# VectorE's attention loop turned at unit 6 of a group instead of at the group's end

## The chip, the cores and the metric

The kernel runs on one core of a Trainium2 chip. A NeuronCore has engines that run programs of their own and meet through semaphores: TensorE (PE in the profile; matmuls and transposes, PEld its weight loads), VectorE (DVE), ScalarE (ACT), GpSimd (POOL) and SyncE (SP, which issues DMAs). The metric is the device time of one launch in microseconds; less is better.

## The reference, cut to what matters

```python
x = x + _L0_cond_ref(...)     # a 32x32 weight picked per batch
x = x + _L1_cond_ref(...)     # base weight, bias, a LoRA adapter per batch
x = x + _L2_cond_ref(...)     # attention, below
x = x + _L3_cond_ref(...)     # as L0
...
def _L2_cond_ref(x, Wq, Wk, Wv, Wo, q_norm_w, k_norm_w, k_cache, v_cache, block_table, cache_seqlens):
    q, k = _rope(_rmsnorm(q, q_norm_w), pos), _rope(_rmsnorm(k, k_norm_w), pos)
    k_all = jnp.concatenate([k_cache[block_table], k], axis=1)   # 512 cached + 32 own rows
    v_all = jnp.concatenate([v_cache[block_table], v], axis=1)
    scores = jnp.einsum('bqhd,bkhd->bhqk', q, k_all) * SCALE
    probs = jax.nn.softmax(jnp.where(valid, scores, -1e30), axis=-1)
    o = jnp.einsum('bhqk,bkhd->bqhd', probs, v_all)
    return jnp.einsum('bse,de->bsd', o, Wo)
```

x is 64 batches of 32 rows by 512. There are 32 query heads and 8 key/value heads of 128; four query heads with 32 rows each share a key head, which makes 128 rows of scores.

## The kernel before

The stages run one after the other: the first two residual steps, the projections (v, then q and k, to about 720 us of the trace), the attention (about 720 to 2090 us), and the second half of the output projection with the last residual step.

**The attention** is a pipeline over units. One unit is one batch and one key head: 64 batches by 8 heads are 512 units. A group is four batches, 32 units (UG), and there are 16 groups (NT), 0 to 15. Every engine has its own list of `step(g, u)` calls. Each engine writes group 0 out, loops over groups 1 to 14, and writes group 15 out. PE, ACT and DVE turn their loops after unit 31. POOL's loop runs from unit 24 to unit 23 of the next group (ROT). SP's body is one call of `group`. SP reaches its turn when units 2 and 3 of the next group are being worked on, since it waits for outputs of the group's last batch.

For unit n of a group, DVE's step n does, in this order: `split_k` for unit n+3 (the low part of the keys, k_lo, L999), `masked_max` for n+2 (L1013, L1014; nmx), `inverse` (L1020) and `normalise` (L1025, L1026) for n+1, and at some units a mask (L991), a q split (L1005), the low part of the outputs (`heads_low`, L1031), and at unit 31 the residual sum (L1037). PE's step n computes scores of n+2 (L1247), which need k_lo of n+2 and the maximum of n. It turns the probabilities of n (L1134), which needs DVE's L1026 of that unit, and multiplies with the values of n-1 (L1280, with L1290 at the end of a batch). ACT's step n does the exponential of n+1 (L744), the high part of the keys of n+4 (k_hi, L730), and the copy of the turned probabilities (L790). After each batch come L768, L751 and L753.

**SP** loads the key pages of batch b+2 into the buffer of batch b as soon as DVE has made the last k_lo of batch b: it waits at L445, then issues own keys (L383), reads 16 page numbers and issues 16 loads of 128 KB (L378). The queries (L387) go ahead of these. Then come own values (L392), the store of outputs (L456) and, in the fourth batch, x2's store (L465). ACT's L730 is the first to read the pages, four units ahead of PE.

Waits are on counters that count on through the program, so the place of a loop's turn changes no dependency.

Of the kernel before, what the change touches and what calls it, by code (L numbers as in the profile page):

```python
# [43 lines left out]
UG = BT * HK  # L44
# [13 lines left out]

HEADS_AT = {2: (1, 3, 0), 5: (1, 0, 1), 6: (1, 1, 1), 8: (1, 2, 1), 10: (1, 3, 1), 18: (0, 0, 0), 21: (0, 1, 0), 26: (0, 2, 0)}
RESIDUAL = UG - 1  # L60
WO_SPLIT = 8

SCALE = 1.0 / float(np.sqrt(D))
# [16 lines left out]
def build(nc, x, cond_row, id_row, bt_row, idx_pages, seq_tok, seq_all, w0, w3, wb, bias,  # L80
# [3 lines left out]
    with ctx:  # L84
# [224 lines left out]
        def _(sp):  # L309
# [9 lines left out]
            def load_b(i, j):  # L319

                i, j, t = tile(i, j)
                _, rows = nc.values_load_multi_w_load_instructions(
                    ids[0:1, bass.ds(t * BT, BT)], engines=SP, min_val=0, max_val=LORAS - 1)
                for b in range(BT):
                    sp.dma_start(b4[j][b * RANK:(b + 1) * RANK, :],
                                 lora_b[bass.ds(rows[b], 1)].rearrange("a r n -> r (a n)")).then_inc(s_bin[j], 16)
# [47 lines left out]
            def load_pages(table, par, first=0, count=NPP):  # L374

                _, pages = nc.values_load_multi_w_load_instructions(table, engines=SP, min_val=0, max_val=PAGES - 1)
                for n in range(count):
                    sp.dma_start(k_sb[par][:, first + n, :, :].rearrange("p h t -> p (h t)"),  # L378
                                 kT_cache[bass.ds(pages[n], 1)].rearrange("a p n -> p (a n)")).then_inc(s_k[par], 16)
# [229 lines left out]
        def _(act):  # L609
# [160 lines left out]
            def split_wo(half, h, raw):  # L770

                if h == 0:
                    act.wait_ge(s_wo_in, 16 * half + 16)
                at = slice(h * T, (h + 1) * T)
                nc.scalar.copy(wo_hi[:, at], raw[:, at]).then_inc(s_wohi, 1)

            def step(g, u):
                n = g * UG + u
                fixed = isinstance(n, int)
                if u % HK == 0 and not (fixed and n == 0):  # L780
                    own_turned(g * BT + (u // HK - 1))
                if u % HK == 1 and not (fixed and n == 1):
                    out_heads(*((g, u // HK - 1) if u > 1 else (g - 1, BT - 1)))
                if not (fixed and n + 1 >= NU):
                    exps(n + 1, u + 1)
                if u % HK != 1 and not (fixed and n + 4 >= NU):
                    split_k(n + 4, u + 4, g * 2 + (u + 4) // (2 * HK))
                act.wait_ge(s_ta, n + 1)
                ge(act, s_pv, n - 1)
                nc.scalar.copy(pT_sb[u % 2], pT).then_inc(s_evA, 1)  # L790
                if u % HK == 1 and not (fixed and n + 4 >= NU):
                    split_k(n + 4, u + 4, g * 2 + (u + 4) // (2 * HK))
                if u % 4 == 3 and not (fixed and n + 5 >= NU):
                    split_q(g * (UG // 4) + (u // 4 + 2), u + 5, g * 2 + (u + 5) // (2 * HK))
                if u in HEADS_AT:
                    back, b, half = HEADS_AT[u]
                    if not (fixed and g < back):
                        heads_high(g - back, b, half)
# [18 lines left out]
            for u in range(UG):  # L817
                step(0, u)
                if 0 <= u - WO_SPLIT < H2:
                    split_wo(0, u - WO_SPLIT, wo_raw)  # L820
            with act.Fori(1, NT - 1) as g:
# [32 lines left out]
        def _(dve):  # L854
# [134 lines left out]
            def make_mask(b):  # L989

                nc.vector.tensor_scalar(mask[:, 0:L], iota[:], seqf[:, bass.ds(b, 1)], NEG, ALU.is_ge, ALU.mult)\  # L991
                    .then_inc(s_mask, 1)

            def split_k(n, u):

                b, h = u // HK % 2, u % HK
                dve.wait_ge(s_khi, n + 1)
                lo, hi = (k[u % 2].rearrange("p (s t) -> p s t", t=PSIZE) for k in (k_lo, k_hi))
                nc.vector.tensor_tensor(lo, k_sb[b][:, :, h, :], hi.bitcast(F32), ALU.subtract).then_inc(s_klo, 1)  # L999

            def split_q(m, u):

                b, h, i = u // HK % 2, u % HK, u // 4 % 2
                dve.wait_ge(s_qhi, m + 1)
                nc.vector.tensor_tensor(q_lo[i], q_sb[b][:, h * P:h * P + HW], q_hi[i].bitcast(F32), ALU.subtract)\  # L1005
                    .then_inc(s_qp, 1)

            def masked_max(n, u, b):

                if u % HK == 0:  # L1010
                    dve.wait_ge(s_mask, b + 1)
                dve.wait_ge(s_qk, n + 1)
                nc.vector.memset(hold[:, u % 4:u % 4 + 1], 0.0)  # L1013
                nc.vector.tensor_tensor_reduce(  # L1014
                    out=p_sb[u % 4], in0=scores, in1=mask[:], scale=-SCALE, scalar=3e38,
                    op0=ALU.add, op1=ALU.min, accum_out=nmx[:, u % 4:u % 4 + 1]).then_inc(s_mx, 1)

            def inverse(n, u):
                dve.wait_ge(s_exp, n + 1)
                nc.vector.reciprocal(rinv[:, u % 4:u % 4 + 1], rs[:, u % 4:u % 4 + 1]).then_inc(s_ri, 1)  # L1020

            def normalise(n, u):
                dve.wait_ge(s_ri, n + 1)
                p, j = p_sb[u % 4], u % 4
                nc.vector.tensor_scalar(po_sb[u // 4 % 4][:, j * C:(j + 1) * C], p[:, L:KW], rinv[:, j:j + 1], None, ALU.mult)  # L1025
                nc.vector.tensor_scalar(p[:, 0:L], p[:, 0:L], rinv[:, j:j + 1], None, ALU.mult).then_inc(s_p, 1)  # L1026

            def heads_low(g, b, half, count):

                dve.wait_ge(s_hi, g * 8 + count)  # L1030
                nc.vector.tensor_tensor(heads_of(oT_lo, b, half), raw_of(b, half), heads_of(oT_hi, b, half).bitcast(F32),  # L1031
                                        ALU.subtract).then_inc(s_lo, 1)

            def residual(g):
                dve.wait_ge(s_wo, g + 1)
                dve.wait_ge(s_x2r, g * 16 + 16)
                nc.vector.tensor_tensor(x2r, yP, x2r, ALU.add).then_inc(s_x2y, 1)  # L1037

            def split_wo(half, h, lo, raw):

                dve.wait_ge(s_wohi, half * H2 + h + 1)
                at = slice(h * T, (h + 1) * T)
                nc.vector.tensor_tensor(lo[:, at], raw[:, at], wo_hi[:, at].bitcast(F32), ALU.subtract).then_inc(s_wolo, 1)

            def step(g, u):
                n = g * UG + u
                fixed = isinstance(n, int)
                if not (fixed and n + 3 >= NU):
                    split_k(n + 3, u + 3)
                if not (fixed and n + 2 >= NU):  # L1050
                    masked_max(n + 2, u + 2, g * BT + (u + 2) // HK)
                if not (fixed and n + 1 >= NU):
                    inverse(n + 1, u + 1)
                    normalise(n + 1, u + 1)
                if u % HK == 5 and not (fixed and n + 3 >= NU):
                    make_mask(g * BT + (u // HK + 1))
                if u % 4 == 0 and not (fixed and (n == 0 or n + 4 >= NU)):
                    split_q(g * (UG // 4) + (u // 4 + 1), u + 4)
                if u - 1 in HEADS_AT:
                    back, b, half = HEADS_AT[u - 1]  # L1060
                    if not (fixed and g < back):
                        heads_low(g - back, b, half, HI_COUNT[b, half])
                if u == RESIDUAL and not (fixed and g == 0):
                    residual(g - 1)
# [16 lines left out]
            for u in range(UG):  # L1081
                if u == 4:
                    for j in range(2):
                        dve.wait_ge(s_qst[j], 16 * QKB * NT // 2)
                step(0, u)
                if 0 <= u - WO_SPLIT < H2:
                    split_wo(0, u - WO_SPLIT, wo_lo, wo_raw)
            with dve.Fori(1, NT - 1) as g:
                for u in range(UG):
                    step(g, u)  # L1090
            for u in range(UG):
                step(NT - 1, u)
            for u in list(HEADS_AT)[:5]:
                heads_low(NT - 1, *HEADS_AT[u][1:], HI_COUNT[HEADS_AT[u][1:]])
# [337 lines left out]
```

## Time and profile before

| | us |
|---|---|
| median of 3 runs | 2311.89 |
| lowest, highest | 2305.17, 2313.61 |
| the profiled execution, its own time | 2306.23 |
| its span, first to last instruction | 2304.4 |
| PE busy | 2231.9 (97%) |
| DVE busy | 1754.5 (76%) |
| ACT busy | 1598.8 (69%) |

The mean granted clock was 0.996 of full speed. Busy time of PE counts from a modelled end of pipelined matmuls. A timeline row gives start, duration, engine, line, operation, tiles, count, and in brackets the idle time of the engine ahead of it and what ended it; "issue" means that nothing the profile shows was waited for.

### The profile page before, as it was taken

The page shows a single profiled execution, that of the slowest core. Times are in us where ns is not written, and L with a number is a line of the kernel's source. Part 1 is how long each engine was busy: PE and PEld are TensorE (multiplying, and loading weights), DVE is VectorE, ACT ScalarE, POOL GpSimd, SP SyncE. Part 2 cuts the span into 40 slices and gives each one's busy share as a digit, 9 for nine tenths or more (in the row PEclk, how much of TensorE's full clock was granted, in tenths as well). Part 3 has the DMA queues.
Part 4 walks back from the last instruction along what each step waited for, and adds up shares of the span by engine and source line. Part 5 has one row for each costly group of instructions (what it writes and reads, how often), then busy time and mean ns, then how long its engine had stood idle before and what let it go on. Part 6 is the DMA issues. An engine that isn't in the chain of part 4 may idle for free.

```text
span 2304.4 us, 57131 instructions
## 1 busy us (share of the span) xinstructions
PE 2231.9 (97%) x15424; PEld 2001.3 (87%) x15424; DVE 1754.5 (76%) x5602; ACT 1598.8 (69%) x4413; POOL 598.2 (26%) x907
## 2 busy tenths in 40 slices
PE   7999999999999899999999999999999999998999
PEld 6787888888888899999999999999999999997777
DVE  3434777777778998988888888898898898995332
ACT  4423666666667988888888888888888788884221
POOL 1003444444443322222222222222222222220000
PEclk9999999999999999999999999999999999999999
DMA  5335333333337887877887877887887877864332
GB/s 170 95 114 165 102 101 102 100 101 118 101 92 251 249 255 249 260 250 249 260 252 246 258 251 244 256 257 241 256 255 246 259 254 252 256 223 179 137 123 96
DMA packets 348202, 456.58 MB, mean 198 GB/s; under 512 B 34682, under 2 KB 281018, under 8 KB 343870
## 3 DMA queue, kind: packets, MB, share of 16 engines
q1 hardware_dynamic: 308430, 315.83, 44.5%
q0 software_dynamic: 36864, 134.23, 17.4%
q10 hardware_dynamic: 2672, 4.31, 0.5%
q14 instruction: 202, 1.65, 0.3%
q8 instruction: 34, 0.56, 0.1%
HBM read 374.54 MB, written 79.69 MB: 197 GB/s over the span
## 4 chain that ended last, share of the span: by engine, by line
PE 80%; DVE 9%; issue 7%; ACT 2%; DMA 1%; ACTq 0%; DVEq 0%; SPq 0%
PE oP L1280 14%; PE S L1247 13%; PE S L1204 12%; PE oP L1204 11%; PE S L1298 8%; PE bank L1134 7%; PE bank L1311 6%; DVE k_lo L999 3%; PE oP L1134 3%; PE oP L1162 2%; DVE regC L1026 1%; PE oP L1290 1%; DVE q_lo L1005 1%; PE oP L1154 1%; PE oP L1368 1%
## 5 line engine op out<-in xcount | busy, mean ns | idle before, releaser
L1280 PEld LDWEIGHTS oP<-regC,regK 128*128 128x128 f32 x4096 | 530.8, 192 | 32.1 <-issue 1.1
L1280 PE MATMUL oP<-regC,regK 128*128 128x128 f32 x4096 | 540.8, 275 | 0.1
L730 ACT CAST k_hi<-regK 128x544 fp32r<-128x544 f32 x512 | 331.3, 647 | 130.4 <-PE S L1247 130.1
L1014 DVE CUSTOM_DVE_ANT_0 regC<-S,mask 128x544 f32<-128x544 f32 x512 | 368.9, 721 | 62.9 <-issue 56.8
L999 DVE TENSOR_TENSOR k_lo<-regK,k_hi 128x544 fp32r<-128x544 f32 x512 | 368.6, 720 | 38.1 <-ACT k_hi L730 32.6
L744 ACT ACTIVATE regC<-regC,nmx 128x544 f32<-128x544 f32 x512 | 387.2, 756 | 3.4 <-DVE nmx L1014 2.9
L548 POOL COPY idx<-idx_all 128x1 int32 (+1 forms) x260 | 65.7, 255 | 993.3 <-PE oP L1290 648.4
L1134 PE MATMUL bank<-ident,regC 128*128 128x128 f32 x2048 | 308.9, 274 | 12.7 <-DVE regC L1026 12.7
L790 ACT COPY regC<-bank 128x512 f32<-128x512 f32 x512 | 297.7, 582 | 29.2 <-PE bank L1134 29.2
L569 POOL TENSOR_TENSOR regC<-regC 128x256 f32<-128x256 f32 x320 | 245.4, 787 | 275.3 <-DVE regC L974 275.3
L551 POOL DMA_INDIRECT regK<-v_cache,idx x256 | 272.3, 1064 | 118.9 <-issue 118.1
L1247 PE MATMUL S<-k_hi,q_hi 128*128 128x288 f32 (+1 forms) x1024 | 256.3, 331 | 29.0 <-DVE nmx L1014 28.5
L1134 PEld LDWEIGHTS bank<-ident,regC 128*128 128x128 f32 x2048 | 243.5, 141 | 15.7 <-DVE regC L1026 15.5
L1026 DVE TENSOR_SCALAR regC<-regC,rinv 128x512 f32<-128x512 f32 x512 | 246.8, 482 | 0.0
L1247 PE MATMUL S<-k_hi,q_lo 128*128 128x288 f32 (+1 forms) x1024 | 214.1, 290 | 0.0
L1247 PE MATMUL S<-k_lo,q_hi 128*128 128x288 f32 (+1 forms) x1024 | 213.1, 289 | 0.0
L1247 PEld LDWEIGHTS S<-k_hi,q_hi 128*128 128x128 f32 x1024 | 155.5, 192 | 45.8 <-DVE k_lo L999 23.0
L974 DVE SCALAR_TENSOR_TENSOR regC<-oP,rstd,regK 128x128 f32<-128x128 f32 x640 | 172.8, 343 | 8.3
L974 DVE SCALAR_TENSOR_TENSOR regC<-S,rstd,regK 128x128 f32<-128x128 f32 x640 | 172.8, 344 | 8.2
L1204 PE MATMUL S<-w_hi,x2T_hi 128*128 128x512 f32 x384 | 157.6, 410 | 1.8 <-ACT regC L681 1.8
L1247 PEld LDWEIGHTS S<-k_hi,q_lo 128*128 128x128 f32 x1024 | 158.1, 190 | 0.0
L1204 PE MATMUL oP<-w_hi,x2T_hi 128*128 128x512 f32 x384 | 157.3, 410 | 0.0
(138 smaller groups left out, 4296.1 us busy)
## 6 DMA issues: line engine op xcount, KB each, us to landing
regK<-kT_cache SPq DMA_DIRECT2D x1024, 128.0 KB
qkT_d<-regC SPq DMA_DIRECT2D x160, 256.0 KB, 2.3
regC<-qkT_d SPq DMA_DIRECT2D x64, 512.0 KB, 6.7
oT_d<-regC SPq DMA_DIRECT2D x64, 256.0 KB
regK<-oT_d SPq DMA_DIRECT2D x16, 1024.0 KB, 5.2
regC<-wqk SPq DMA_DIRECT2D x10, 1024.0 KB, 5.2
v_d<-regC SPq DMA_DIRECT2D x32, 256.0 KB, 2.3
regK<-qkT_d SPq DMA_DIRECT2D x64, 128.0 KB
```

Source lines behind the costliest of these rows:

```text
L551: nc.gpsimd.indirect_dma_start(out=v_sb[par][:, m, :], out_offset=None, in_=v_cache, in_offset=bass.IndirectOffsetOnAxis(ap=idx[k][:, m:m ...
L730: nc.scalar.copy(k_hi[u % 2].rearrange("p (s t) -> p s t", t=PSIZE), k_sb[b][:, :, h, :]).then_inc(s_khi, 1)
L744: nc.scalar.activation(p, p, ACT.Exp, bias=nmx[:, u % 4:u % 4 + 1], scale=-1.0, accum_out=rs[:, u % 4:u % 4 + 1]).then_inc(s_exp, 1)
L790: nc.scalar.copy(pT_sb[u % 2], pT).then_inc(s_evA, 1)
L974: last = nc.vector.scalar_tensor_tensor(out=dst[t % 2][:, h, :], in0=bank[t % 4][:, h * D:(h + 1) * D], scalar=rstd[:, t % 4, h:h + 1], in ...
L999: nc.vector.tensor_tensor(lo, k_sb[b][:, :, h, :], hi.bitcast(F32), ALU.subtract).then_inc(s_klo, 1)
L1014: nc.vector.tensor_tensor_reduce(out=p_sb[u % 4], in0=scores, in1=mask[:], scale=-SCALE, scalar=3e38, op0=ALU.add, op1=ALU.min, accum_out= ...
L1026: nc.vector.tensor_scalar(p[:, 0:L], p[:, 0:L], rinv[:, j:j + 1], None, ALU.mult).then_inc(s_p, 1)
L1134: last = nc.tensor.transpose(dst[:, c * P:(c + 1) * P], src[:, c * P:(c + 1) * P], ident[:])
L1204: last = nc.tensor.matmul(bank[t % 4], a[:, c, rows], w[k][:, cols], start=(c == 0 and m == 0), stop=(c == HC - 1 and m == 2))
L1247: last = nc.tensor.matmul(scores[:, at], q[u // 4 % 2][:, head], k[u % 2][:, at], start=(i == 0), stop=(i == 2))
L1280: last = nc.tensor.matmul(oP[:, at:at + P], v_sb[b][:, m, h * D:(h + 1) * D], pT_sb[u % 2][:, m * P:(m + 1) * P], start=(h < 4 and m == 0) ...
```

## The change

DVE's loop is turned at unit 6. The first six units of group 1 are written out ahead of the loop. The loop's body, still run 14 times, is now units 6 to 31 of group g and then units 0 to 5 of group g+1. Units 6 to 31 of group 15 follow it. Every step is executed once, as before and in the same order. No other engine's program changes.

```diff
+TURN = 6
...
+            for u in range(TURN):
+                step(1, u)
             with dve.Fori(1, NT - 1) as g:
-                for u in range(UG):
+                for u in range(TURN, UG):
                     step(g, u)
-            for u in range(UG):
+                for u in range(TURN):
+                    step(g + 1, u)
+            for u in range(TURN, UG):
                 step(NT - 1, u)
```

In the program as built, with register, wait and branch instructions counted, DVE's loop body goes from 308 to 310 instructions, and it starts 46 instructions further on (the six written units). All of DVE's code ahead of that is the same.

The head of DVE's attention loop before (the branch enters it; the ISA row behind it computes registers, the two ISA rows of L1014 are the masked maximum and the read of its result):

```order
L1088 UNCONDITIONAL_BRANCH
L1088 ISA
L999 TENSOR_TENSOR k_lo_69<-regK,k_hi_70 128x544
L1012 REGISTER_ALU
L1013 MEMSET hold 128x1
L1014 ISA regC,nmx<-S,mask 128x544
L1014 ISA nmx 128x1
L1019 REGISTER_ALU
L1020 RECIPROCAL rinv<-rs 128x1
L1025 TENSOR_SCALAR regC<-regC,rinv 128x32
```

The same place in DVE's program now, at unit 6 (lines are 1 to 3 higher; the rows ahead of the branch are unit 5 of group 1):

```order
L1026 TENSOR_SCALAR regC<-regC,rinv 128x32
L1027 TENSOR_SCALAR regC<-regC,rinv 128x512
L992 TENSOR_SCALAR mask<-iota,seqf 128x512
L1091 UNCONDITIONAL_BRANCH
L1091 ISA
L1000 TENSOR_TENSOR k_lo_69<-regK,k_hi_70 128x544
L1012 ISA
L1013 REGISTER_ALU
L1014 MEMSET hold 128x1
L1015 ISA regC,nmx<-S,mask 128x544
```

The loop starts with the k_lo of unit 9 instead of unit 3, and has one register instruction more at its head.

The tail of DVE's loop before, with the backward branch behind the residual sum of unit 31:

```order
L1025 TENSOR_SCALAR regC<-regC,rinv 128x32
L1026 TENSOR_SCALAR regC<-regC,rinv 128x512
L1036 ISA
L1037 TENSOR_TENSOR regC<-bank,regC 128x512
L1088 REGISTER_ALU
L1088 COMPARE_AND_BRANCH
```

And now, with the backward branch behind the mask of unit 5:

```order
L1027 TENSOR_SCALAR regC<-regC,rinv 128x512
L992 ISA
L992 TENSOR_SCALAR mask<-iota,seqf 128x512
L1091 REGISTER_ALU
L1091 COMPARE_AND_BRANCH
```

The step from unit 31 to unit 0, which had the branch, is now straight code in the middle of the body.

## Rows read from the trace of the kernel before

**Rows 1.** The page, section 4: the chain that ended last, by engine.
```profile
PE 80%; DVE 9%; issue 7%; ACT 2%; DMA 1%; ACTq 0%; DVEq 0%; SPq 0%
```

**Rows 2.** Waits from 894 to 2006 us: engine line waited for: us in total, times, longest.
```profile
PE S L1247 <- DVE nmx L1014: 20.2, 25, 1.7
...
DVE regC L1025 <- issue: 16.6, 12, 2.0
...
PE bank L1134 <- DVE regC L1026: 12.7, 13, 1.6
...
DVE k_lo L999 <- issue: 5.5, 2, 2.9
```

**Rows 3.** Waits from 811 to 893 us (group 1); the view has no row of PE there.
```profile
DVE k_lo L999 <- ACT k_hi L730: 0.6, 3, 0.2
```

**Rows 4.** Timeline of ACT: L768 as groups 1, 2 and 15 begin.
```profile
811.75 0.37 ACT L768 COPY regC<-bank 128x256 f32<-128x256 f32 x1
...
894.46 0.37 ACT L768 COPY regC<-bank 128x256 f32<-128x256 f32 x1 [0.20 <-PE bank L1264]
...
2006.79 0.37 ACT L768 COPY regC<-bank 128x256 f32<-128x256 f32 x1
```

**Rows 5.** Timeline of DVE where its loop turns into group 5.
```profile
1150.77 0.68 DVE L1037 TENSOR_TENSOR regC<-bank,regC 128x512 f32<-128x512 f32 x1
1153.78 0.73 DVE L999 TENSOR_TENSOR k_lo<-regK,k_hi 128x544 fp32r<-128x544 f32 x1 [2.33 <-ACT k_hi L730]
...
1156.46 0.24 DVE L1025 TENSOR_SCALAR regC<-regC,rinv 128x32 f32<-128x32 f32 x1 [1.22 <-issue]
```

**Rows 6.** Timeline of DVE at the same units in straight code, group 14 to 15.
```profile
2006.40 0.68 DVE L1037 TENSOR_TENSOR regC<-bank,regC 128x512 f32<-128x512 f32 x1
2007.00 0.72 DVE L999 TENSOR_TENSOR k_lo<-regK,k_hi 128x544 fp32r<-128x544 f32 x1
```

**Rows 7.** Timeline of ACT where its loop turns into group 5.
```profile
1149.93 0.58 ACT L790 COPY regC<-bank 128x512 f32<-128x512 f32 x1
1150.40 0.62 ACT L738 CAST q_hi<-regC 128x512 fp32r<-128x512 f32 x1
```

**Rows 8.** DMA queues, 362 to 465 us: packets, MB, share of 16 engines.
```profile
q14 instruction: 10, 0.08, 0.3%
```

**Rows 9.** DMA queues, 980 to 1066 us (one group of the loop).
```profile
q14 instruction: 10, 0.08, 0.5%
```

**Rows 10.** Timeline of PE at the turn into group 5, and leaving the loop.
```profile
1150.74 0.38 PE L1264 MATMUL bank<-ident,regC 128*128 128x128 f32 x2
1151.13 0.52 PE L1247 MATMUL S<-k_hi,q_hi 128*128 128x288 f32 x2
...
2006.37 0.38 PE L1264 MATMUL bank<-ident,regC 128*128 128x128 f32 x2
2006.53 0.49 PE L1247 MATMUL S<-k_hi,q_hi 128*128 128x288 f32 x2
```

**Rows 11.** Timeline of SP in group 5.
```profile
1163.28 0.36 SPq L387 DMA_DIRECT2D regC<-qkT_d  x1
1164.92 0.35 SPq L383 DMA_DIRECT2D regK<-qkT_d  x1
```

**Rows 12.** Line L378, 1164 to 1186 us: ns min/median/max, first and last start.
```profile
L378 SPq DMA_DIRECT2D regK<-kT_cache x16: 332/333/342, 1170.8 to 1178.8; - x16
```

**Rows 13.** The page, section 6: issues, KB each, median us to landing.
```profile
qkT_d<-regC SPq DMA_DIRECT2D x160, 256.0 KB, 2.3
regC<-qkT_d SPq DMA_DIRECT2D x64, 512.0 KB, 6.7
```

**Rows 14.** Timelines of DVE (unit 7's k_lo), ACT and DVE (unit 12's keys), group 5.
```profile
1164.04 0.72 DVE L999 TENSOR_TENSOR k_lo<-regK,k_hi 128x544 fp32r<-128x544 f32 x1
...
1185.34 0.65 ACT L730 CAST k_hi<-regK 128x544 fp32r<-128x544 f32 x1 [0.16 <-PE S L1247]
...
1187.34 0.72 DVE L999 TENSOR_TENSOR k_lo<-regK,k_hi 128x544 fp32r<-128x544 f32 x1
```

## The prediction

> **What bounds the kernel now.** The chain of waits lies on PE for 80% of the span, but 16% of it is DVE and "issue" [rows 1]. So I looked for the places where PE waits. In the list of waits of the loop's stretch, 894 to 2006 us, PE idles 20.2 us for DVE's maximum and 12.7 us for DVE's probabilities, 32.9 us together; the latter comes 13 times, once for each time that the loop turns [rows 2]. Group 1 is the loop's first run, reached from straight code and not by the backward branch; there PE waits for no engine at all, and DVE's waits for ACT's k_hi are 0.6 us in all [rows 3].
>
> The same stands in the length of the groups. From one L768 to the next, group 1 takes 894.46 - 811.75 = 82.71 us. The thirteen groups behind it, each with a turn at its head, take 2006.79 - 894.46 = 1112.33 us, 85.56 each [rows 4]. The excess is 1112.33 - 13 x 82.71 = 37.1 us, 2.85 a turn. That is all there is to win at the turns.
>
> Next, who loses it. At the turn DVE ends the residual sum at 1151.45 and starts k_lo only at 1153.78, 2.33 us later. Some work follows without a gap, then L1025 waits another 1.22 us for nothing that the profile shows [rows 5]. The view puts the first gap down to ACT's k_hi. I don't take that: where the same units follow in straight code, k_lo comes 0.60 us after the start of the residual sum, with no gap [rows 6]. So there are two stops of DVE's own, 3.55 us in all, of which PE feels about 2.85. The other engines' turns show what a turn needn't cost: ACT branches in the same place and its work runs on [rows 7].
>
> **Why DVE stops, and what the change does to that.** The instruction queue q14 serves DVE, ACT, POOL and SP. It moves ten packets of 8 KB in a group of the loop [rows 9]. The loop bodies, in instructions as the trace records them, are DVE 308, SP 429, ACT 260, POOL 70. Suppose that a packet is a block of 128 instructions, that an engine holds four blocks, and fetches the next block on entering one. Then a body that lies in three blocks, plus the one fetched ahead, stays in place, and one that lies in four is fetched anew at each turn, five blocks with the one ahead. DVE and SP make ten, ACT and POOL none: the row. In the q and k projection DVE's body has 402 instructions and ACT's 399; neither fits three blocks, POOL and SP do, and again ten packets pass in one turn of DVE's loop [rows 8]. Blocks of 256 would give at most eight in this second place. ACT's 260 instructions cover at least three blocks, and its turn is free [rows 7], so four blocks are held.
>
> The second stop fixes where the blocks lie. Between the loop's start and the L1025 that stops there are eight instructions (the first order rows of the change). So the loop began with the last eight of a block, and covered 8 + 128 + 128 + 44: four blocks. The change puts 46 instructions ahead of it. It now starts 46 - 8 = 38 into a block and ends at 38 + 310 = 348, under 384: three blocks. By the count above it then stays in place, as ACT's does, and both stops go, at every turn.
>
> The Trainium skill ("Runtime: NRT & Kernel Launch", Instruction fetch mechanics) states it otherwise: blocks of 256 instructions, two of them held, prefetch in sequence, and a stall at a taken branch whose target is no longer held. By it the 310 instructions fill both blocks and the one fetched ahead drives out the first; the sum would be that of the first rival below. This trace's packets, and ACT's free turn with 260 instructions, speak against it.
>
> **The change part by part.**
> Removed: both stops, up to 37.1 us with all that follows from them.
> Moved: DVE's branch, to behind the mask of unit 5. No row shows a held turn of DVE's attention loop. The nearest is ACT's, whose next work starts before the work ahead of it has ended (1150.40 against 1149.93 + 0.58) [rows 7]: 0. At most it costs the 0.2 us that ACT waits behind its own turn [rows 4], 13 x 0.2 = 2.6. I take 0, since DVE's sequencer has the mask's time as cover. A gain here is excluded, since a branch does no work.
> Added: two register instructions a turn, and straight code once for 46 instructions. DVE's sequencer runs ahead of the engine, as in the head of the loop, where register instructions fall into running work: 0.
> Stays: PE's own branch. From L1264 to L1247 it takes 0.39 us at the turn and 0.16 where the loop is left [rows 10]: 0.23 x 13 = 3.0 us of the 37.1 remain.
> Turned up: SP, which DVE's stops covered. SP's turn lies just ahead of L387 at 1163.28 [rows 11] and hangs on ACT's outputs of the batch ahead, not on DVE's stops. SP is through with L387 at 1163.64 and issues L383 at 1164.92, 0.16 behind the end of DVE's k_lo of unit 7 at 1164.76 [rows 11, 14]. So it waited 1.1 us for that k_lo. With the stops gone k_lo is 2.6 us earlier (2.85 less 0.23), SP's loads only 1.1, while ACT wants the keys 2.6 earlier: the loads lose 1.5 us of room. How much room is there? The last page load is issued at 1178.8 [rows 12]; landing takes somewhere between 2.3 and 6.7 us by loads of 256 and 512 KB [rows 13]; ACT reads at 1185.34 and waits for PE, not for a DMA [rows 14]. That is 0 to 4.2 us of room. At no room, ACT's k_hi would be 1.5 late. DVE takes it up 1.35 us after it is made (1187.34 - 1185.99) [rows 14], so 0.15 us would get through: 13 x 0.15 = 2 us. With 2 us of room, nothing. I take 0.5 us for the whole.
>
> **The sum.** 37.1 - 3.0 - 0.5 = 33.6 us. It is near the 32.9 that PE waits for DVE in the list. On the profiled execution: 2306.2 - 33.6 = 2272.6 us. That execution is 5.7 below the median of the runs; against the median: 2311.9 - 33.6 = **2278 us**. Own range: a gain of 30 (all the costs above) to 37, on runs that spread from 2305 to 2314: 2268 to 2284.
>
> **The rivals.**
> *One stop stays.* DVE holds fewer blocks than ACT's turn suggests, or fetches further ahead. Then the target is gone at the branch, and only the second stop vanishes, since the next block's edge is 90 instructions off. Gain: the 12.7 us of PE's waits for probabilities up to DVE's 16.6 [rows 2]: 2295 to 2299. The skill's rule gives this one. Against it: the ten packets, twice.
> *The keys come late.* The room is nil and DVE's 1.35 us of cover is not there, because ACT, blocked, also holds back its copy for PE. Then 1.5 us of each 2.6 return as a wait of ACT for a DMA at the keys of unit 12: gain 13 x 1.1 = 14, 2298 us. For it: the loads take most of a batch's time already. Against it: in the whole attention no wait for key pages is listed.
> *Nothing.* The two stops belong to the turn whatever its place (I have the blocks wrong). They move to unit 6: 2312.
> *Slower.* They move to unit 6, and cost more there. The residual sum of 0.68 us, which covered the first, is ahead of the branch no longer, only the mask of 0.48; and PE passes on the whole 3.55 instead of 2.85. That is 0.7 + 0.2 = 0.9 a turn, 12 us: 2324. With fetches as slow as the worst seen, 2.9 and 2.0 instead of 2.33 and 1.22 [rows 2], another 1.35 a turn: 2341. It decides if the body still lies in four blocks and a block's edge follows the branch closely, for which my count would have to be off by more than 36 instructions.
>
> **How the numbers follow.** Forecast 0.80; one stop stays 0.09; keys late 0.05; nothing 0.03; slower 0.03. The range reaches from the forecast's low end to the two rivals with a small gain: 2268 to 2299. A change of 0.5% is 11.6 us, about what a measurement of this kernel can tell. The forecast lies beyond it, and most of the next two: 0.80 + 0.06 + 0.04 = 0.90 faster. Within it: the rest of those two and nothing, 0.07. Slower 0.03.
>
> **What the profile after would show.** If right: q14 moves five packets a group instead of ten; no idle time of DVE ahead of the k_lo that opens the loop's body, nor ahead of the one that follows the residual sum; groups of 82.9 to 83.1 us; PE's waits for DVE gone from the list. If one stop stays: five packets remain DVE's and a gap of 2.3 us stands ahead of the first k_lo behind the branch. If the keys are late: ACT's L730 waits for a DMA once a group, at unit 8. I would be wrong altogether if groups stay at 85.6 us.

## The result, and the profile after

| | before | after |
|---|---|---|
| median of the runs of one comparison, us | 2312.75 | 2274.53 |
| lowest, highest | 2305.17, 2315.96 | 2271.54, 2278.96 |
| the profiled execution, its own time | 2306.23 | 2276.92 |
| its span | 2304.4 | 2275.1 |
| PE busy | 2231.9 (97%) | 2229.5 (98%) |
| DVE busy | 1754.5 (76%) | 1757.3 (77%) |
| ACT busy | 1598.8 (69%) | 1595.5 (70%) |

The ratio of the runs is 0.9833, with a 95% interval of 0.9809 to 0.9858: 38 us less. 2278 was forecast. In a second comparison, with nine runs of the kernel before, it was 0.9834 (0.9813 to 0.9855).

The page of the kernel after. First the chain that ended last, which answers to [rows 1]; then the instruction queue for the whole execution (packets, MB, share of 16 engines), which had 202 packets before:

```profile
PE 92%; DVE 2%; issue 2%; SPq 2%; DMA 1%; ACT 1%; ACTq 0%; DVEq 0%
```
```profile
q14 instruction: 137, 1.12, 0.2%
```

The 65 packets that are gone are five for each of 13 turns. In one group of the loop, 980 to 1066 us, the DMA queues now show half of [rows 9]:

```profile
q14 instruction: 5, 0.04, 0.2%
```

All waits of PE, ACT on a DMA, and DVE's k_lo from 894 to 1975 us (engine, line, what was waited for: us in total, times, longest), answering to [rows 2]. The lines of the code are 1 to 5 higher than before: k_lo is L1000, the scores L1252, the turned probabilities L1139, k_hi L731.

```profile
DVE k_lo L1000 <- ACT k_hi L731: 9.8, 40, 2.4
ACT k_hi L731 <- DMA regK<-kT_cache: 7.5, 7, 4.0
PEld oP L1285 <- issue: 3.8, 13, 0.3
PEld S L1252 <- issue: 3.1, 13, 0.3
PEld bank L1139 <- issue: 2.7, 1, 2.7
ACT regC L769 <- PE bank L1269: 2.6, 13, 0.2
PE bank L1139 <- ACT regC L791: 2.6, 1, 2.6
```

PE's waits for DVE, 32.9 us before, are no longer there. One wait of PE, 2.6 us, is new (the 2.7 us of its weight loads are the same wait); it belongs to a late key page and is taken up below.

DVE at its new turn, the mask of unit 5 and the k_lo that opens the body (timeline: start, duration, engine, line, operation, tiles). In [rows 5] 2.33 us lay ahead of that k_lo, and 1.22 us ahead of the first normalisation (now L1026):

```profile
996.26 0.48 DVE L1027 TENSOR_SCALAR regC<-regC,rinv 128x512 f32<-128x512 f32 x1
996.66 0.48 DVE L992 TENSOR_SCALAR mask<-iota,seqf 128x512 f32<-128x512 f32 x1
997.05 0.72 DVE L1000 TENSOR_TENSOR k_lo<-regK,k_hi 128x544 fp32r<-128x544 f32 x1
997.70 0.72 DVE L1015 CUSTOM_DVE_ANT_0 regC<-S,mask 128x544 f32<-128x544 f32 x1
...
998.54 0.24 DVE L1026 TENSOR_SCALAR regC<-regC,rinv 128x32 f32<-128x32 f32 x1
```

And at the old place, from unit 31 to unit 0, now straight code, as in [rows 6]:

```profile
1149.69 0.69 DVE L1038 TENSOR_TENSOR regC<-bank,regC 128x512 f32<-128x512 f32 x1
1150.29 0.72 DVE L1000 TENSOR_TENSOR k_lo<-regK,k_hi 128x544 fp32r<-128x544 f32 x1
```

ACT's L769 as groups 1, 2 and 15 begin, which answers to [rows 4]:

```profile
815.71 0.37 ACT L769 COPY regC<-bank 128x256 f32<-128x256 f32 x1
...
898.81 0.37 ACT L769 COPY regC<-bank 128x256 f32<-128x256 f32 x1 [0.20 <-PE bank L1269]
...
1978.67 0.37 ACT L769 COPY regC<-bank 128x256 f32<-128x256 f32 x1
```

The thirteen groups take 1978.67 - 898.81 = 1079.9 us instead of 1112.3: 32.4 us less. Twelve take 82.8 to 82.9 us each, one 85.60. The spans differ by 29.3 us only, because this execution needed 4 us more ahead of group 1, which begins at 815.71 instead of 811.75.

### The profile page after: what moved, and what is told of

Read it like the earlier page. It is cut to its first block, busy times and chain, and to the rows that moved or that the text cites. A ratio compares the mean times of both kernels' runs of the same rounds, so it can differ in the third digit from the quotient of the medians.

```text
span 2275.1 us, 57159 instructions
## 1 busy us (share of the span) xinstructions
PE 2229.5 (98%) x15424; PEld 1999.8 (88%) x15424; DVE 1757.3 (77%) x5602; ACT 1595.5 (70%) x4413; POOL 600.0 (26%) x907
## 4 chain that ended last, share of the span: by engine, by line
PE 92%; DVE 2%; issue 2%; SPq 2%; DMA 1%; ACT 1%; ACTq 0%; DVEq 0%
PE oP L1285 18%; PE S L1252 16%; PE S L1209 12%; PE oP L1209 11%; PE bank L1139 9%; PE S L1303 8%; PE bank L1316 7%; PE oP L1139 3%; PE oP L1167 2%; PE oP L1295 2%; SPq L379 1%; PE oP L1159 1%; DVE k_lo L1000 1%; PE oP L1373 1%; PE bank L1269 1%
## 5 line engine op out<-in xcount | busy, mean ns | idle before, releaser
L731 ACT CAST k_hi<-regK 128x544 fp32r<-128x544 f32 x512 | 331.5, 647 | 127.7 <-PE S L1252 118.9
L1000 DVE TENSOR_TENSOR k_lo<-regK,k_hi 128x544 fp32r<-128x544 f32 x512 | 368.6, 720 | 12.7 <-ACT k_hi L731 12.7
L549 POOL COPY idx<-idx_all 128x1 int32 (+1 forms) x260 | 70.3, 273 | 963.2 <-PE oP L1295 652.0
L1139 PE MATMUL bank<-ident,regC 128*128 128x128 f32 x2048 | 307.3, 272 | 2.8 <-ACT regC L791 2.8
L1252 PE MATMUL S<-k_hi,q_hi 128*128 128x288 f32 (+1 forms) x1024 | 256.7, 332 | 8.8 <-DVE nmx L1015 8.4
L1139 PEld LDWEIGHTS bank<-ident,regC 128*128 128x128 f32 x2048 | 243.6, 141 | 3.3 <-issue 3.3
L1252 PE MATMUL S<-k_hi,q_lo 128*128 128x288 f32 (+1 forms) x1024 | 213.8, 290 | 0.0
L1252 PE MATMUL S<-k_lo,q_hi 128*128 128x288 f32 (+1 forms) x1024 | 212.8, 289 | 0.0
L1252 PEld LDWEIGHTS S<-k_hi,q_hi 128*128 128x128 f32 x1024 | 155.1, 191 | 23.4 <-issue 9.5
L1252 PEld LDWEIGHTS S<-k_hi,q_lo 128*128 128x128 f32 x1024 | 157.8, 189 | 0.0
L1252 PEld LDWEIGHTS S<-k_lo,q_hi 128*128 128x128 f32 x1024 | 157.5, 189 | 0.0
```

The costliest lines, as they stand in the source:

```text
L731: nc.scalar.copy(k_hi[u % 2].rearrange("p (s t) -> p s t", t=PSIZE), k_sb[b][:, :, h, :]).then_inc(s_khi, 1)
L1139: last = nc.tensor.transpose(dst[:, c * P:(c + 1) * P], src[:, c * P:(c + 1) * P], ident[:])
L1252: last = nc.tensor.matmul(scores[:, at], q[u // 4 % 2][:, head], k[u % 2][:, at], start=(i == 0), stop=(i == 2))
```

## The experiments

There are twelve runs: eleven further kernels, and the changed kernel once more (e11). In some the code of DVE's attention loop is only shifted: one-element memsets of an unused tensor stand in DVE's last block of the q and k projection, where DVE has idle time. The edit, in every kernel with a PAD, is this one; its lines move up by up to 5.

```diff
+PAD = 46
...
+        spare = sb("spare", [P, 48])
...
                 for t in range(NT):
                     rotate(e, t, table)
+                    if buf is None:
+                        for n in range(t * PAD // NT, (t + 1) * PAD // NT):
+                            nc.vector.memset(spare[n // 48 * 64:n // 48 * 64 + 64, n % 48:n % 48 + 1], 0.0)
```

The offset is the place of the loop's first instruction in a block of 128, worked out as in the prediction; the end is offset plus body. "Stop" is the idle time of DVE ahead of the k_lo that opens the body, and "packet" the time from the stop's start to that of the first q14 packet in it, medians of the 13 turns. "Packets a group" counts q14 from one group's start to the next. "Group" is the mean of groups 2 to 14.

| kernel | turn behind unit | offset, end | packets a group | stop, us | packet, us | group, us | median, us |
|---|---|---|---|---|---|---|---|
| before | 31 | 120, 428 | 10 | 2.28 | 0.35 | 85.56 | 2316.10 |
| e1, before + 46 | 31 | 38, 346 | 5 | none | - | 83.11 | 2277.96 |
| e2, before + 90 | 31 | 82, 390 | 10 | 2.59 | 0.55 | 84.51 | 2296.77 |
| e3, after + 60 | 5 | 98, 408 | 10 | 4.41 | 2.50 | 88.94 | 2347.37 |
| e4, after + 82 | 5 | 120, 430 | 10 | 3.90 | 2.00 | 89.37 | 2361.75 |
| e5, TURN 14 | 13 | 102, 410 | 10 | 3.66 | 1.61 | 86.51 | 2328.94 |
| e6, TURN 8 + 47 | 7 | 102, 411 | 10 | 2.33 | 0.39 | 84.22 | 2287.43 |
| e7, after + 36 | 5 | 74, 384 | 5 | none | - | 83.31 | 2280.02 |
| e8, after + 37 | 5 | 75, 385 | 10 | 5.64 | 2.62 | 90.22 | 2365.87 |
| e9, e8, gathers cut | 5 | 75, 385 | 10 | 3.87 | 0.75 | 87.72 | 2334.38 |
| e10, e8, key pages cut | 5 | 75, 385 | 10 | 4.93 | 1.90 | 89.39 | 2361.15 |
| e11, after | 5 | 38, 348 | 5 | none | - | 82.84 | 2271.59 |
| e12, after, SP turned | 5 | 38, 348 | 6 | none | - | 82.86 | 2271.14 |

The kernel before had medians of 2316.1, 2317.3 and 2310.2 in the comparisons of e1 to e4, e5 to e8 and e9 to e12. e7 and e8 have one run each, e9 and e10 two. e12's sixth packet is SP's: by the trace its body now has 431 instructions instead of 429, and DVE's body is that of e11.

### e1 to e4: the body's place in the blocks, or the place of the turn?

The change moved both. e1 moves the code and leaves the turn where it was.

> The kernel before, with DVE's loop turned after unit 31 as before; the only edit is 46 one-element memsets of an unused tensor, spread over the 16 tiles of DVE's last block of the q and k projection, where DVE has idle time. Nothing is left out. The loop's code then starts 46 instructions later, at the same distance as in the changed kernel: offset 38 of a block of 128, body 308, end 346, three blocks. Theory (the body has to lie in three blocks, the place of the turn is nothing): both of DVE's stops go, q14 moves 5 packets a group, groups 2 to 14 take 82.9 to 83.1 us each, and the time is 2271 to 2282, as the changed kernel. Rival (the place of the turn does it: at unit 6 it has cover, at unit 31 it has none): 10 packets a group, stops of 2.3 and 1.2 us ahead of the first k_lo and of the first normalisation, and 2306 to 2316 as before.

Measured: 2277.96 us, ratio 0.9831 (0.9804 to 0.9859), the same as the change. The timeline of DVE at the turn behind unit 31, where [rows 5] had the stop:

```profile
1149.83 0.69 DVE L1042 TENSOR_TENSOR regC<-bank,regC 128x512 f32<-128x512 f32 x1
1150.43 0.72 DVE L1004 TENSOR_TENSOR k_lo<-regK,k_hi 128x544 fp32r<-128x544 f32 x1
```

The stop is gone with the turn in its old place. So the gain comes from where the body lies; that the place of the turn adds anything isn't to be seen.

> As the run before it, with 90 memsets: offset 82, end 390, four blocks, and the next edge of a block is 46 instructions behind the loop's start. Nothing is left out. Theory: the body is fetched anew at each turn, 10 packets a group, but the second stop (an edge 8 instructions behind the start) isn't there, since the fetch of the next block has the time of 46 instructions (about 8 us). The first stop of 2.3 us ahead of the first k_lo stays. A turn then costs the first stop as far as PE feels it: group length 84.0 to 84.9 us, time 2289 to 2301. Rival (an edge near the loop's start is what costs, not the number of blocks): no stop at all, about 2275. Rival (fetches cost the same wherever the edges are): 2306 to 2316.

Measured: 2296.77 us, ratio 0.9915 (0.9889 to 0.9941). DVE at the same turn:

```profile
1150.49 0.69 DVE L1042 TENSOR_TENSOR regC<-bank,regC 128x512 f32<-128x512 f32 x1
1154.04 0.73 DVE L1004 TENSOR_TENSOR k_lo<-regK,k_hi 128x544 fp32r<-128x544 f32 x1 [2.86 <-issue]
1154.69 0.72 DVE L1019 CUSTOM_DVE_ANT_0 regC<-S,mask 128x544 f32<-128x544 f32 x1
...
1155.53 0.38 DVE L1030 TENSOR_SCALAR regC<-regC,rinv 128x32 f32<-128x32 f32 x1
```

One stop without the other, as the theory had it: ahead of the normalisation (L1030) there is none. The first stop is worth 2296.8 - 2278.0 = 18.8 us, the second 2316.1 - 2296.8 = 19.3 (18 and 14 by the group lengths of one profile each). Here the view calls the stop "issue"; in [rows 5] it had named ACT's k_hi for the same thing.

```diff
-PAD = 46
+PAD = 90
```

> The changed kernel (turn at unit 6) with 60 such memsets: offset 98, body 310, end 408, four blocks, the next edge 30 instructions behind the loop's start. Nothing is left out. Theory: q14 back to 10 packets a group; a stop of about 2.3 us ahead of the k_lo that opens the body, now at unit 6, and none behind it. 2291 to 2303. Rival (at unit 6 the turn is covered): 5 or 10 packets, no stop that PE feels, 2271 to 2282.

Measured: 2347.37 us, ratio 1.0128 (1.01 to 1.0156), 44 us over the end of the expected range. The ten packets and the single stop are there, but the stop is far longer. DVE at the turn behind unit 5:

```profile
1178.35 0.48 DVE L997 TENSOR_SCALAR mask<-iota,seqf 128x512 f32<-128x512 f32 x1
1183.10 0.72 DVE L1005 TENSOR_TENSOR k_lo<-regK,k_hi 128x544 fp32r<-128x544 f32 x1 [4.27 <-issue]
```

> The changed kernel (turn at unit 6) with 82 such memsets: offset 120, body 310, end 430, the next edge 8 instructions behind the loop's start, as in the kernel before but with the turn at unit 6. Nothing is left out. Theory: both stops are back, at unit 6: 10 packets a group, about 2.3 us ahead of the first k_lo and 1.2 us about eight instructions behind it. With the shorter cover there (a mask of 0.48 us instead of a residual sum of 0.68 ahead of the branch) 2306 to 2326. Rival (the place of the turn does it): 2271 to 2282.

Measured: 2361.75 us, ratio 1.0198 (1.0171 to 1.0225). The second stop is back as well, ahead of the reciprocal, eight instructions behind the start, and the time is 36 us over the end of the expected range and 14 us over e3 (6 by the groups). In group 5 of e4:

```profile
1186.91 0.16 DVE L1026 RECIPROCAL rinv<-rs 128x1 f32<-128x1 f32 x1 [1.29 <-ACT regC L747]
```

The view names ACT's exponential; in e3 the same reciprocal follows without a gap. The packets and the stops came where they were expected, but both times lay far above their ranges: the price of a turn that doesn't fit is not the same everywhere. That opened a question of its own.

### e5 and e6: what a stop costs, by the place of the turn

In every stop the trace shows q14's packet, and DVE starts again 1.55 to 1.76 us behind the end of what was fetched for it (medians of the nine kernels with stops; in e8, e9 and e10 that is the second packet of two). What varies is when the packet moves: 0.35 us into the stop behind unit 31, 2.5 us behind unit 5. A unit's place in its batch of eight sets what else is under way: GpSimd issues the four value gathers of a batch (queue q0) at units 2 to 5 of it. POOL's last gather ahead of the stops, first of e3, then of e6 (run with the turn behind unit 7):

```profile
1175.17 0.97 POOL L554 DMA_INDIRECT regK<-v_cache,idx  x1 [0.50 <-issue]
```
```profile
1159.16 0.96 POOL L554 DMA_INDIRECT regK<-v_cache,idx  x1 [0.50 <-issue]
```

The stop of e3 begins at 1178.8, 3.7 us behind the start of that issue; that of e6 at 1167.6, 8.4 us behind it.

```diff
-TURN = 6
+TURN = 14
```

> The changed kernel with DVE's turn at unit 14 of a group instead of 6, with no padding: offset 102, body 308, end 410, four blocks, the next edge 26 instructions behind the start. Nothing is left out. The run with the turn at unit 6 and 60 memsets took 2347, far over what was expected: its stop ahead of the k_lo at the body's head was 3.7 to 5.3 us, not 2.3. In the trace the fetch's packet went 1.9 to 3.5 us after the stop's start there, and 0.1 to 1.1 us in the run with the turn at unit 31, and only at unit 6 were queue q0's gathers (GpSimd's value pages) still moving. Theory (the fetch comes behind the value gathers of the batch, which run once per batch, so eight units on it is the same): a stop of 3.7 to 5.3 us at unit 14, 10 packets a group, 2340 to 2352. Rival (unit 6 has a collision of its own that comes once a group, such as SP's turn shortly ahead of it): a stop of 2.0 to 2.9 us, 2290 to 2305. Rival (it fits all the same, the blocks are counted wrongly): 2271 to 2282.

Measured: 2328.94 us (2317.78 to 2340.93 over ten runs), ratio 1.0056 (1.0035 to 1.0077). The stops, 2.75 to 4.22 us, reach from near those of unit 31 to those of e3. So the place once a group isn't what makes them long, but eight units on it isn't quite the same either: the expectation held by half.

```diff
-TURN = 6
+TURN = 8
...
+PAD = 47
```

> The changed kernel with the turn at unit 8, so behind unit 7 of the group, which has the same place in its batch as unit 31 in its own; 47 memsets bring the loop to offset 102, body 309, end 411, as in the run with the turn at unit 14. Nothing is left out. Theory (what the stop costs hangs on the phase in the batch, by the value gathers that are then under way): 10 packets a group, a stop of 2.0 to 2.9 us ahead of the first k_lo, as with the turn at unit 31, 2289 to 2305. Rival (the last units of a group are cheap for another reason, such as the residual sum as cover): 2335 to 2352.

Measured: 2287.43 us, ratio 0.988 (0.9851 to 0.991), two us under the expected range. Two units behind e3, with a body that doesn't fit either, the time is 60 us less.

Part of these 60 us is TensorE's clock. PE's wait for DVE's maximum in e3, 894 to 2040 us, is 4.1 us a turn:

```profile
PE S L1257 <- DVE nmx L1020: 53.1, 13, 5.0
```

The group is 88.94 - 82.84 = 6.1 us longer than without a stop, 2 us more. The stretches of e3's stop in group 5 (us, busy time and count of PE, PEld, DVE, ACT, POOL, then PE's granted clock, DMA share, GB/s):

```profile
1179.00:1181.00 2.00, 1.78 (x14) 1.50 (x12) 0.00 (x0) 1.44 (x3) 0.00 (x0) 1.00 0.86 312
1181.00:1183.00 2.00, 0.00 (x0) 0.00 (x0) 0.00 (x0) 0.00 (x0) 0.00 (x0) 1.00 0.19 74
1183.00:1185.00 2.00, 0.38 (x3) 0.41 (x4) 1.87 (x7) 0.49 (x1) 0.00 (x0) 0.99 0.61 164
1185.00:1187.00 2.00, 2.00 (x10) 2.00 (x10) 1.96 (x8) 1.08 (x4) 0.00 (x0) 0.50 0.85 259
1187.00:1189.00 2.00, 2.00 (x13) 1.90 (x13) 1.55 (x4) 1.02 (x2) 0.00 (x0) 0.65 0.85 247
```

PE idles 3.84 us here, and when it works again it is granted 0.50 of full speed, 1.2 instead of 2.4 GHz, for about 3 us. All 13 turns of e3 show a mean clock of 0.51 to 0.72 in the 6 us behind k_lo, which, as an estimate, is 1.7 us or more lost in each (6 x 0.28). In e6 all 13 show 1.00. e5 has both. Its turns in groups 6 and 7, PE at the first scores behind the stop:

```profile
1279.99 0.37 PE L1252 MATMUL S<-k_hi,q_hi 128*128 128x288 f32 x1 [2.52 <-DVE nmx L1015]
```
```profile
1366.66 0.49 PE L1252 MATMUL S<-k_hi,q_hi 128*128 128x288 f32 x2 [3.39 <-DVE nmx L1015]
```

and the granted clock behind each of them (same columns as above):

```profile
1281.00:1283.00 2.00, 2.00 (x19) 1.96 (x18) 1.96 (x8) 1.85 (x4) 0.00 (x0) 1.00 0.69 211
```
```profile
1368.00:1370.00 2.00, 2.00 (x10) 1.90 (x9) 1.96 (x7) 1.66 (x3) 0.00 (x0) 0.50 0.77 223
```

In e5 the clock fell at the four turns where PE idled 3.12 to 3.39 us, and not at the nine where it idled 2.96 or less. The four groups took 87.8 to 88.1 us, the others 85.2 to 87.1. The profile is of the shortest of e5's ten runs. The mean granted clock that is recorded for each run goes from 0.994 in that one to 0.985 in the longest; 0.009 of 2330 us is 21 us, nearly the whole spread of 23. So it seems that more turns fall this way in the longer executions; no profile shows it turn by turn.

### e7 and e8: one instruction

> The changed kernel with 36 memsets: offset 74, body 310, end 384, the last instruction of the third block. Nothing is left out. Theory (three blocks stay, and the edges lie where the second stop placed them): 5 packets a group and no stop, 2271 to 2282. Rival (two and a half blocks or less are held, or the edge lies a few instructions earlier): 10 packets and 2340 to 2355.

> The changed kernel with 37 memsets: offset 75, body 310, end 385: the backward branch alone lies in a fourth block. Nothing is left out. Theory: 10 packets a group, a stop of 3.7 to 5.3 us a turn, 2335 to 2350, 60 to 75 us more than with one memset less. Rival (edges lie some instructions later, or nothing sharp happens): 2271 to 2282.

Measured: 2280.02 and 2365.87 us. One memset more, and with it the backward branch alone in a fourth block, costs 86 us, by one run of each; e8 lies 16 us over its expected range. The instruction queue of the two pages, e7 and then e8:

```profile
q14 instruction: 137, 1.12, 0.2%
```
```profile
q14 instruction: 202, 1.65, 0.2%
```

The edge lies exactly where the second stop of [rows 5] had placed it. The Trainium skill ("Runtime: NRT & Kernel Launch", Instruction fetch mechanics) has blocks of 256 instructions, two of them held. The trace disagrees: one instruction adds 65 packets of 8 KB, an odd five a turn, which blocks of twice that size wouldn't give, and a body of 310 that ends at 384 goes free. Its rule that a taken branch out of what is held has to wait for a fetch does agree, at 2.3 to 5.6 us.

e8's stops are longer than e3's (5.64 against 4.41) for a reason that the trace shows too: in e8 two packets follow each other in the stop, the second 0.9 us long, and DVE starts behind both. A reading that fits, but that no run tests by itself: entering the fourth block, whose only instruction is the branch, sets off the fetch of a fifth, which nobody needs, ahead of the target's.

### e9 and e10: which traffic holds the fetch back

Queue q0 moves GpSimd's value gathers, q1 what SP issues, here the key pages. The stop of e8 in group 3 began at 1002.0. The DMA queues from 1001 to 1003 us and from 1003 to 1005 us:

```profile
q0 software_dynamic: 92, 0.36, 54.7%
q1 hardware_dynamic: 64, 0.26, 36.5%
```
```profile
q1 hardware_dynamic: 182, 0.32, 43.1%
q0 software_dynamic: 41, 0.11, 18.9%
q14 instruction: 2, 0.02, 3.8%
```

q14's packets move, from 1004.1 on, when the burst of q0 is nearly over. Both experiments start from e8; each cuts one kind of traffic to a quarter.

```diff
-                gather_v((k + 2) % 4, k % 2, m)
+                gather_v((k + 2) % 4, k % 2, m, 32)
...
-                    out=v_sb[par][:, m, :], out_offset=None, in_=v_cache,
+                    out=v_sb[par][0:r, m, :], out_offset=None, in_=v_cache,
```

> The run with 37 memsets (four blocks, turn at unit 6, 2366, stops of 4.9 to 7.2 us, the packet of the fetch starting 2.1 to 4.3 us after the stop) with one edit: in the attention GpSimd's value gathers of queue q0 bring 32 of the 128 rows of each page group; the other rows keep older values, so that part of the values is left out. Theory (the fetch comes behind the gathers): the packet starts at 0.1 to 1.5 us after the stop, the stop falls to 3.1 to 4.4 us (two packets, one of them 0.9 long, and 1.6 from its end to the restart), and the time to 2300 to 2325. Rival (the traffic of the key pages does it): no change, 2350 to 2370. The rest of the kernel is bound by PE and should not gain by smaller gathers.

Measured: 2334.38 us; stops of 3.55 to 4.26 us (median 3.87, from 5.64), packets at 0.75 us instead of 2.62. The stop and the packet are where they were expected; the time fell by 31 us and ended 9 over the expected range. The range had left out the clock: PE still idles 3.1 to 3.8 us a turn, and behind nine of the 13 the clock fell. Those nine groups took 87.9 to 89.1 us, the other four 86.1 to 86.8. The length of PE's idle time alone doesn't tell which: the clock fell behind 3.21 us and was kept behind 3.65.

```diff
-                        load_pages(btab[0:1, k * NPP:(k + 1) * NPP], k % 2)
+                        load_pages(btab[0:1, k * NPP:(k + 1) * NPP], k % 2, r=32)
```

> The counterpart: 37 memsets, gathers whole, but the 16 key page loads of each batch (queue q1) in the attention bring 32 of the 128 partitions; the other rows keep older keys, so that part of the keys is left out. Theory (the fetch comes behind the gathers): stops of 4.5 to 7 us stay, 2345 to 2368. Rival (the key pages do it, or the whole load on the DMA engines): stops of 3.1 to 4.4 us, 2300 to 2325.

Measured: 2361.15 us; stops of 4.17 to 5.75 us (median 4.93), packets at 1.90 us. Cutting the gathers gives back 31 us and brings the packet forward by 1.9 us. Cutting the key pages brings it forward by 0.7 us, by one profile each; the 5 us between the times are no more than what the kernel before differs by between the two comparisons (2317.3 and 2310.2), so a gain in time isn't shown. The gathers are what mainly holds the fetch back. Key pages alone don't do it behind unit 31, where q1 is in full use while the packet moves (kernel before, 1151 to 1153 us):

```profile
q1 hardware_dynamic: 517, 0.47, 81.2%
q14 instruction: 1, 0.01, 2.2%
```

The Trainium skill ("DMA: Bandwidth & Descriptors", Queues, rings and completion order) says that a DMA engine takes its queues in turn, a packet of each. By that alone a fetch would pass the gathers after a packet or so, and e3 would cost no more than e2, an estimate of 2297 us; it took 2347. Whether the fetch is asked for late or waits in the DMA engines can't be told: the trace shows when a packet moves, not when it was asked for.

### e11 and e12: the late key pages

In the profiled execution after, ACT's k_hi of unit 12 waited for its keys seven times, and once this passed through to PE. ACT in group 4:

```profile
1099.90 0.65 ACT L731 CAST k_hi<-regK 128x544 fp32r<-128x544 f32 x1 [3.95 <-DMA regK<-kT_cache]
```

e12 turns SP's loop between its third and fourth batch, away from the loads for unit 12:

```diff
-            with sp.Fori(1, NT - 1) as g:
-                group(g, False, False)
+            group(1, False, False, (0, 1, 2))
+            with sp.Fori(1, NT - 2) as g:
+                group(g, False, False, (3,))
+                group(g + 1, False, False, (0, 1, 2))
+            group(NT - 2, False, False, (3,))
```

> The changed kernel as it is, beside the next run on the same chip. 2271 to 2282. In the profiled run of it ACT's k_hi waited 7 times for the key pages of unit 12 (in all 7.5 us), and once (4.0 us) this reached PE, for 2.7 us; here again 1 to 3 groups should be 1.5 to 4 us longer than 82.86.

> The changed kernel with SP's loop turned as well: SP's body now starts with the fourth batch of a group and ends with the third of the next, so that SP's turn lies between the third and the fourth batch's loads and no longer ahead of the loads for unit 12. Nothing is left out; no wait changes. Theory (the late key pages are what is left of the turn of SP): no group of 2 to 14 over 83.1 us, no wait of ACT for key pages at unit 12, 2 to 6 us less than the run beside it, so a ratio to it of 0.9975 to 0.999. Rival (the pages are late by chance of the DMA traffic, whatever SP does, or SP's own fetch moves the delay to another batch): no difference, waits at another unit in place of those.

Measured: 2271.59 (2270.43 to 2275.39) and 2271.14 (2269.98 to 2272.22): no difference. The change itself showed no late group this time. Its waits for key pages in the loop, and the longest, were

```profile
ACT k_hi L731 <- DMA regK<-kT_cache: 1.5, 3, 0.6
```

and e12 had none. So the small waits are gone in e12, as the theory said, but they cost nothing in e11, and the gain of 2 to 6 us wasn't there to be had. In the four profiles with SP's turn unmoved and DVE's stops gone (after, e1, e7, e11) the 13 groups together take about 2.7, 3.2, 5.9 and 0 us more than at 82.86 each; the long groups in them are those with a late key page. One profile of e12 can't tell whether moving SP's turn prevents the large ones.

## Why the prediction was right, point by point

**The cause.** Right, and shown as far as the place of the body goes. Both stops belong to a body that lies in four blocks of 128 instructions: e1 takes them away without moving the turn, e4 brings them back with the turn moved, and e7 and e8 put the limit between 384 and 385, with five packets a turn gone or back. That four blocks are held and the next one is fetched ahead is the count that fits all of these; the trace shows packets, not what an engine holds.

**The whole of what there is to win, 37.1 us.** The group of e11, 82.84 us, is 0.13 over group 1's 82.71 [rows 4]; 13 x (85.56 - 82.84) = 35.4 us were won where no key page was late, and 32.4 in the first profile after.

**PE's own turn, 3.0 us.** The row is as forecast, 0.39 us from L1269 to L1252 at the turn into group 5:

```profile
1149.65 0.38 PE L1269 MATMUL bank<-ident,regC 128*128 128x128 f32 x2
1150.04 0.52 PE L1252 MATMUL S<-k_hi,q_hi 128*128 128x288 f32 x2
```

and 0.16 leaving the loop, as in [rows 10]. But of 0.23 a turn only 0.13 to 0.15 stay in the group's length (82.84 in e11, 82.86 in e12): 2 us, not 3.

**DVE's new turn, 0.** Right: k_lo follows the mask at 0.39 us, with no gap.

**SP's turn turned up, 0.5 us.** Right in kind, too small. SP's and ACT's rows of group 5 after, against [rows 11, 14]:

```profile
1163.03 0.35 SPq L384 DMA_DIRECT2D regK<-qkT_d  x1
```
```profile
1182.22 0.65 ACT L731 CAST k_hi<-regK 128x544 fp32r<-128x544 f32 x1 [0.67 <-DMA regK<-kT_cache]
```

Counted from PE's turn, the loads are issued 0.8 us earlier and not 1.1, and ACT wants its keys 2.7 earlier: the room falls by 1.9 us, not 1.5. The prediction reckoned with a fixed landing time, so that all groups would be the same. In fact most groups have just enough, and single ones are up to 4 us late. The term is 0 to 5.9 us by execution, 3 in the mean of four.

**The sum.** 33.6 us forecast, 32.4 and 35.4 measured in the loop. The medians differ by 38. That is 3 to 6 us more than the profiles give; the profiled execution before was among the shortest of its kind (2306.2, where its runs reach to 2322.6). In it, one group of 87.25 us had PE's clock at 0.80 in the 6 us behind the turn. The longer ones have no profile, but the mean granted clock of each run is on record: in the 29 runs of the kernel before beside the experiments it is 0.995 to 0.997 in those up to 2310.5 us and 0.987 to 0.993 in those from 2315.9 us on; in the changed kernel's nine it is 0.995 to 0.998. As an estimate, the 0.004 between 0.993 and 0.997 is 9 us of 2310. So part of what the change gives back at the median is very likely PE's clock behind DVE's stops. The prediction has no such term: it took its 33.6 us from the profile of a short execution and subtracted them from the median, which may be why it falls short of the 38 there. The range was wide enough to hold the difference.

**One stop stays, 2295 to 2299.** It didn't happen, but e2 is this case made on purpose: 2296.8.

**Slower, 2324 to 2341.** e4 is this case: 2361.75, 21 us over the range's end. The step that failed is the one that moved the fetch's duration unchanged from unit 31 to unit 6 ("fetches as slow as the worst seen"). The fetch takes longest just where the change put the turn, and two things on top weren't reckoned with: the gathers, and PE's clock after 3 to 5 us of idling. The forecast hung on a fit with 36 instructions to spare, and what was behind it was a loss of 49 us (e8 against the kernel before beside it), not of 12 to 29.

## What to carry to other kernels

If an engine that feeds PE stops at each turn of its loop, for nothing that its waits explain, count the packets of the instruction queue per turn and the instructions of the body, and work out in which block of 128 the loop starts. A body that ends by instruction 384, counted from its first block's start, is free here; one instruction more cost 86 us. Padding in idle code is as good a cure as moving the turn, and any edit of code ahead of such a loop can undo it. If a body can't fit, put its turn where no gathers are under way (e6 lost 60 us less than e3 that way), and look at PE's granted clock behind the stop too.

## What the runs showed of the hardware that was not expected

- The restart comes 1.55 to 1.76 us (medians) behind the end of the fetch, in all nine kernels with stops, whose median stops go from 2.28 to 5.64 us. The packet itself takes 0.3 us in e3 and 0.3 to 0.7 in the kernel before; the second of two takes 0.9 us in e8 and 0.7 to 1.0 in e9.
- GpSimd's gathers delay the fetch's packet by about 2 us (2.62 against 0.75 us with three quarters of their rows gone), key pages by 0.7 us (2.62 against 1.90, without a gain in time beyond the spread).
- A stop can cost more than its length, because PE's clock is at 1.2 GHz behind it: in e3 in all 13 turns (PE idle 3.4 to 5.0 us), in e9 in nine (3.2 to 3.8, but kept in four of 3.1 to 3.65), in e5 in four (3.1 to 3.4, but in none of those with up to 2.96), in e6 in none (up to 1.6). It also fell in one turn of the kernel before, where PE had idled 1.73 us, in one of e2 (1.84 us), and once in e7 at 1768 us, where there is no stop of DVE and PE had idled 2.2 us for the late keys.
